# One Trainium2 core, a fused decoder layer: the load queue's order within a round is changed

## The chip, the cores and the metric

The kernel runs on one core of one Trainium2 chip. The metric is the device time of one execution in microseconds (us); of several runs the median is given. The engines are named as in the profile: PE is TensorE, DVE is VectorE, ACT is ScalarE, POOL is GpSimd, SP is SyncE, which here computes nothing and only issues DMA transfers in the order in which its program lists them ("SPq" in the rows).

## What is computed

A decoder layer of pre-norm form over 128 sequences of 64 tokens with 128 features, all in float32:

```python
x = x + self_attention(layernorm(x))        # 16 heads of 8, rotary positions, causal
x = x + cross_attention(layernorm(x), ctx)  # no softmax; followed by its own layer norm
x = x + expert_ffn(layernorm(x))            # 8 experts, each token goes to the one of largest affinity
```

`x` and `ctx` are each 128 x 64 x 128. The self-attention has a softmax. The cross-attention multiplies its unnormalised scores into the values, adds its input, and normalises. The expert layer is 128 -> 512 -> 128 with a ReLU, and its result is gated by a sigmoid.

## The kernel before

**Tiling.** The 8192 tokens are cut into 32 groups (`NG = 32`) of 256 tokens, four sequences each. For the two attentions each group passes through all engines in pieces, and the pieces are software-pipelined by hand: every engine runs a loop of rounds, and in round c it does the piece of group c, another piece of group c-1, and so on back to group c-8. A call `stage(g, k, op)` in a function `one(g)` means "in this round, do `op` for the group k behind". Each engine executes its own list strictly in order; semaphores tie the lists together. Almost every tile has two buffers, used by even and odd groups (`g.par`), so a transfer into a buffer waits until the group two before has finished with it.

After the rounds comes the expert part: 71 blocks of 128 tokens, fetched from a DRAM table sorted by expert.

**The load queue.** SP's list is the subject. In round c it issues, in the version before:

- `load_again` (L519 to L525): group c-4's x a second time, into `xr`, for the residual sum `x1_sum` (DVE, L1514). It waits for `x1_sum` of group c-6.
- `load_x` (L512 to L518): group c's x into `xin`. It waits until ACT's `norm_x` (L1046) of group c-2 has read the buffer. The first reader is DVE's `stats_x` (L1341, shown as `stat_L<-xin`) in DVE's round c.
- `by_head` (L533 to L541): four transfers that copy group c-1's rotated queries and keys `qk` into head slots `ex`. They wait for POOL's `rotated` (L1927, tile `qk`) of group c-1, which is the last piece of POOL's round c. The first reader is PE's `max_scores` (L706).
- `load_ctx` (L526 to L532): group c's context into `cin`. It waits for PE's `ctx_turned` (L782) of group c-2. The first reader is `ctx_turned` of group c.
- then, in `late_loads(c)`, whatever is due once: constants in round 0; ten transfers of biases and cross-attention weights in round 1 (L493 and L495); the mask and four constants in round 4 (L500 to L503); one transfer of 256 KB of expert weights in each of rounds 10 to 25.

**How the rounds of the engines stand.** PE's numbering is one ahead: PE's round c+1 runs beside DVE's, ACT's and POOL's round c (PE does `max_scores` of the group 4 behind, DVE reduces its result 3 behind). One such round is about 14 us long in the middle of the run.

Order on DVE in one round, as far as it matters: `weighted_turned` (L1491), `choose`, `inverse`, two maxima (L1481), small routing steps, `rotate` (L1461), `stats_x` (L1341, `xin`), `x1_sum` (L1514), `stats_x1`, `y_sum` (L1541), `partners` (L1471); then POOL's `rotated`.

Order on PE: `max_scores` (L696, L706), `ctx_turned` (L782), `x_turned` (L664), `values` (L683), ..., `queries_keys` (L673), `max_rows` (L720), `scores` (L738 to L752), `projected` (L800, what `x1_sum` waits for), `attended`, `values_keys`, `cross_output` (L877 to L884), `weighted` (L769). `cross_output` reuses a bank that `x1_sum` of the group behind it has to have read: L877 waits for it.

Two one-time places: PE's `constants()` (L654 to L656, after `queries_keys` of group 1) waits for the ten transfers of SP's round 1 and for masks that ACT makes; and at the end of DVE's round 4 `setup` reduces the mask (L1741, tile `pen`) and waits for its transfer.

Of the kernel before, what the change touches and what calls it, by code (L numbers as in the profile page):

```python
# [144 lines left out]
def decoder_kernel(nc, x, ctx, mask, wself, wcross, bcol, brow, cent, w1t, lngb, b1c, w2t, b2r,  # L145
# [17 lines left out]
    with es:  # L163
# [254 lines left out]
        def stage(g, back, op, *args):  # L418

            if g.back(back).within(NG):  # L420
                op(g.back(back), *args)

        def rounds(one, count, early=None):

            for i in range(count):
                one(Group(i))
                if early:
                    early(i)
# [50 lines left out]
        def _(sp):  # L479
# [61 lines left out]
                    sp.dma_start(ex[g.par][i:P:4, i, :, :], qk[g.par][i:P:4, :, :]).then_inc(d_by[g.par], 16)  # L541

            def one(g):
                stage(g, 4, load_again)
                stage(g, 0, load_x)
                stage(g, 1, by_head)
                stage(g, 0, load_ctx)
            rounds(one, NG + 4, early=late_loads)


# [1618 lines left out]
```

## Time and profile before

| | us |
|---|---|
| median of 3 runs | 671.95 |
| the runs | 669.51, 671.95, 680.21 |
| the profiled execution, device time | 673.08 |
| its span, first to last instruction | 670.6 |
| PE busy in it | 548.1 |

The profiled execution is 1.1 us over the median, and 2.5 us of it lie outside the span. In the profile a bracket behind a row of a timeline gives the engine's idle time just before that row and what released it. PE's rounds from 86 to 465 us are the even part of the run; 0 to 86 us is the filling of the pipeline with the one-time loads; from about 475 us on the expert blocks run.

### The profile page before, as it was taken

To read this page: it belongs to the slowest core of one execution; us is meant where nothing else is said; L and a number is where in the kernel's file an instruction comes from. 1 tells how busy PE (TensorE), PEld (TensorE's weight loads), DVE (VectorE), ACT (ScalarE), POOL (GpSimd) and SP (SyncE) were. 2 spreads that over 40 slices of the span, in tenths; PEclk is the share of its full clock that TensorE was granted. 3 is DMA by queue.
4 is the path that set the end of the run, shared out by engine and by line. 5 is a ranking of instruction groups with operands and counts; after the bars stand their busy time and mean duration, and the time that the engine had idled before them with its cause. 6 is when DMAs were issued, how large, how long until landed. Compare 5 with 4: busy or idle time off the path is not lost.

```text
span 670.6 us, 26792 instructions
## 1 busy us (share of the span) xinstructions
PE 548.1 (82%) x8783; PEld 444.6 (66%) x8783; DVE 490.5 (73%) x1701; ACT 439.2 (65%) x1496; POOL 388.6 (58%) x659
## 2 busy tenths in 40 slices
PE   2284787989998788988889888888788798899995
PEld 1163565767776566665666666666578797799895
DVE  3282698887788777788778887898647676677674
ACT  1343366666676666667567676765567787799894
POOL 1231266676776776766677777675635655555454
PEclk9998799998899998999799999999969998899998
DMA  2215211122222322222222222111211212232220
GB/s 75 75 46 84 53 43 53 59 81 72 67 73 75 108 71 65 67 77 89 90 71 66 74 71 70 51 50 60 70 27 47 56 54 58 79 87 69 60 57 16
DMA packets 61653, 43.85 MB, mean 65 GB/s; under 512 B 17216, under 2 KB 52801, under 8 KB 61520
## 3 DMA queue, kind: packets, MB, share of 16 engines
q1 hardware_dynamic: 56304, 32.84, 17.5%
q0 software_dynamic: 4320, 8.66, 3.9%
q8 instruction: 74, 1.21, 0.8%
q10 hardware_dynamic: 896, 0.66, 0.4%
q14 instruction: 59, 0.48, 0.3%
HBM read 24.46 MB, written 9.74 MB: 51 GB/s over the span
## 4 chain that ended last, share of the span: by engine, by line
PE 39%; DVE 17%; issue 14%; SPq 10%; DMA 8%; POOL 5%; ACT 3%; ACTq 2%; DVEq 2%; another core or an unknown queue 0%; POOLq 0%
DMA xin<-in_x 8%; PE side L970 7%; SPq L541 5%; PE side L955 4%; PE quad L955 4%; PE quad L738 3%; DVE mx L1481 3%; POOL qk L1927 3%; SPq L530 2%; PE quad L752 2%; PE quad L706 2%; PE side L769 2%; DVE x L1514 1%; PE quad L939 1%; PE side L800 1%
## 5 line engine op out<-in xcount | busy, mean ns | idle before, releaser
L2047 POOL DMA_INDIRECT out<-yo,rb x71 | 69.7, 981 | 76.7 <-DVE yo L1808 49.6
L1088 ACT ACTIVATE prob<-quad 128x1024 f32<-128x1024 f32 x64 | 65.6, 1026 | 65.9 <-PE quad L752 65.9
L970 PE MATMUL side<-w,hT 128*128 x568 | 79.0, 284 | 9.9 <-DVE hT L1613 7.1
L2015 POOL DMA_INDIRECT expert_rows<-pay,sli x64 | 64.3, 1004 | 34.4 <-DVE sli L1652 22.2
L970 PEld LDWEIGHTS side<-w,hT 128*128 128x128 f32 x568 | 71.4, 197 | 12.3 <-issue 12.3
L1481 DVE TENSOR_REDUCE mx<-quad 128x16 f32<-128x1024 f32 x64 | 73.9, 1195 | 4.1 <-PE quad L706 3.9
L1916 POOL TENSOR_TENSOR rs_L<-ve_L,half 128x2 f32<-128x2 f32 x32 | 22.3, 698 | 62.6 <-ACT ve_L L1148 62.6
L752 PE MATMUL quad<-shift,pick 32*128 32x128 bf16 x512 | 30.3, 221 | 30.8 <-issue 30.0
L1341 DVE BATCH_NORM_STATS2 stat_L<-xin 128x6 f32<-128x128 f32 x64 | 15.5, 284 | 51.2 <-DMA xin<-in_x 50.9
L1935 POOL TENSOR_TENSOR mt<-mx,mt 128x32 bf16<-128x32 f32 x64 | 14.8, 252 | 53.7 <-ACT mt L1081 53.7
L752 PEld LDWEIGHTS quad<-shift,pick 32*128 32x128 bf16 x512 | 15.8, 92 | 43.9 <-issue 43.6
L1603 DVE TENSOR_SCALAR xh<-rb 128x128 f32<-128x128 f32 x71 | 24.5, 346 | 26.6 <-issue 24.8
L1219 ACT COPY w1b<-w 128x512 f32 x71 | 43.6, 615 | 0.3 <-issue 0.3
L955 PE MATMUL quad<-xhT,w1b 128*128 128x128 f32 x288 | 39.8, 283 | 1.9 <-ACT xhT L1197 1.9
L955 PE MATMUL side<-xhT,w1b 128*128 128x128 f32 x280 | 38.3, 281 | 0.9 <-ACT xhT L1197 0.9
L769 PE MATMUL side<-prob,vau 128*32 128x64 f32 x2048 | 38.1, 229 | 1.1 <-ACT prob L1088 1.0
L738 PE MATMUL quad<-ex,qk 32*64 32x256 f32 x1024 | 35.9, 386 | 3.6 <-issue 2.9
L706 PE MATMUL quad<-ex,qk 32*64 32x256 f32 x1024 | 38.4, 405 | 0.0
L955 PEld LDWEIGHTS quad<-xhT,w1b 128*128 128x128 f32 x288 | 36.5, 199 | 2.1 <-ACT xhT L1197 2.0
L1197 ACT ACTIVATE xhT<-quad,gb 128x128 f32<-128x128 f32 x71 | 33.1, 466 | 7.2 <-PE quad L939 7.0
L683 PE MATMUL side<-ws,xT 128*128 128x128 f32 x128 | 21.2, 290 | 20.1 <-issue 16.0
L673 PE MATMUL side<-xT,ws 128*128 128x256 f32 x128 | 36.9, 413 | 0.6 <-ACT xT L1053 0.6
(280 smaller groups left out, 1737.6 us busy)
## 6 DMA issues: line engine op xcount, KB each, us to landing
ex<-qk SPq DMA_DIRECT2D x128, 64.0 KB
rb<-expert_rows SPq DMA_DIRECT2D x71, 68.0 KB
xin<-in_x SPq DMA_DIRECT2D x32, 128.0 KB
cin<-in_ctx SPq DMA_DIRECT2D x32, 128.0 KB
xr<-in_x SPq DMA_DIRECT2D x32, 128.0 KB
w<-in_w1t SPq DMA_DIRECT2D x8, 256.0 KB
w<-in_w2t SPq DMA_DIRECT2D x8, 256.0 KB
out<-yo,rb POOLq DMA_INDIRECT x71
```

Source lines behind the costliest of these rows:

```text
L673: last = mm(BANK["queries_keys"][:, i * TG:(i + 1) * TG], w, xT[g.par][:, :], start=True, stop=True)
L706: last = mm(quad[64 * b:64 * b + 64, r_, 256 * j:256 * j + 256], qk[g.par][strip, 0, own], ex[g.par][strip, :, 1, own], start=False, stop= ...
L738: mm(quad[64 * b:64 * b + 64, r_, 256 * j:256 * j + 256], qk[g.par][strip, 1, own], ex[g.par][strip, :, 0, own], start=j == 0, stop=False, ...
L752: last = mm(quad[:, r_, :].rearrange("p (j i q) -> p j i q", j=J, i=4)[:, :, i, :], pick[strip, i, :, :].rearrange("p b k -> p (b k)"), sh ...
L769: last = mm(to[32 * i:32 * i + 32, j, :, r_, :], vau[g.par][:, j, 4 * r_ + i, :], prob[g.par][:, r_, (4 * j + i) * SQ:(4 * j + i + 1) * SQ ...
L955: last = mm(HT[u][c // 2][:, (c % 2) * P:(c % 2 + 1) * P], w1b[u][:, c * P:(c + 1) * P], xhT[u][:, :], start=True, stop=True)
L970: last = mm(YB[u][:, 0:D], hT[u][:, c, :], w2[:, bass.ds(e, 1), c, :], start=c == 0, stop=c == FC - 1)
L1088: act(prob[g.par][:, 2 * h_:2 * h_ + 2, :], quad[:, 2 * h_:2 * h_ + 2, :], ACT.Exp).then_inc(*ac_a.done(f"e{h_}"))
L1219: cp(w1b[u][:, :], w1[:, bass.ds(e, 1), :].rearrange("p e f -> p (e f)")).then_inc(*ffn["act_w1"].done("act_w1"))
L1481: v.tensor_reduce(mx[g.par][:, 2 * h_:2 * h_ + 2, :], quad[:, 2 * h_:2 * h_ + 2, :].rearrange("p r (h k) -> p r h k", k=SQ), AX.X, ALU.max ...
L2015: v.indirect_dma_start(out=rows, out_offset=bass.IndirectOffsetOnAxis(ap=sli[g.par][:, j:j + 1], axis=0), in_=pay[g.par][:, j, :], in_offs ...
L2047: v.indirect_dma_start(out=o_rows, out_offset=bass.IndirectOffsetOnAxis(ap=number, axis=0), in_=yo[b.c % 4][:, :], in_offset=None, bounds_ ...
```

## The change

SP's list of a round is put in another order, and two pieces move to another group.

```diff
             def one(g):
+                stage(g, 0, load_x)
+                stage(g, 2, by_head)
+                stage(g, 2, load_ctx)
                 stage(g, 4, load_again)
-                stage(g, 0, load_x)
-                stage(g, 1, by_head)
-                stage(g, 0, load_ctx)
             rounds(one, NG + 4, early=late_loads)
```

In round c the queue now issues x of group c first; then the head-slot transfers and the context of group c-2 (before: c-1 and c); then the second x of group c-4; then what `late_loads(c)` has. No transfer, no wait inside a function and no other engine's list is changed.

## Rows read from the trace of the kernel before

**Rows 1.** The page: busy time, share of the span and instructions of each engine.

```profile
PE 548.1 (82%) x8783; PEld 444.6 (66%) x8783; DVE 490.5 (73%) x1701; ACT 439.2 (65%) x1496; POOL 388.6 (58%) x659
```

**Rows 2.** The page: the chain that ended last, its shares by line.

```profile
DMA xin<-in_x 8%; PE side L970 7%; SPq L541 5%; PE side L955 4%; PE quad L955 4%; PE quad L738 3%; DVE mx L1481 3%; POOL qk L1927 3%; SPq L530 2%; PE quad L752 2%; PE quad L706 2%; PE side L769 2%; DVE x L1514 1%; PE quad L939 1%; PE side L800 1%
```

**Rows 3.** Waits, 80 to 440 us: total us, times, longest.

```profile
DVE stat_L L1341 <- DMA xin<-in_x: 39.6, 20, 3.1
...
PE side L877 <- DVE x L1514: 9.9, 11, 1.3
```

**Rows 4.** Waits of the SP queue, 86 to 480 us.

```profile
SPq L130 <- POOL qk L1927: 264.1, 28, 17.3
```

**Rows 5.** Timeline of SP, start: start us, us issuing, transfer, count.

```profile
3.26 0.43 SPq L516 DMA_DIRECT2D xin<-in_x  x1
22.60 2.44 SPq L541 DMA_DIRECT2D ex<-qk  x4
...
28.60 2.90 SPq L495 DMA_DIRECT2D wop<-in_wself  x4
...
47.01 2.91 SPq L541 DMA_DIRECT2D ex<-qk  x4
...
61.56 0.47 SPq L500 DMA_DIRECT2D mk<-in_mask  x1
```

**Rows 6.** Timeline of PE, start.

```profile
32.94 0.79 PE L654 MATMUL side<-ws,bvx 128*128 128x128 f32 x2 [9.95 <-DMA wop<-in_wself]
...
34.86 2.01 PE L706 MATMUL quad<-ex,qk 32*64 32x256 f32 x32
...
71.76 1.20 PE L683 MATMUL side<-ws,xT 128*128 128x128 f32 x4 [13.15 <-issue]
```

**Rows 7.** Timeline of ACT, start: the last of the masks.

```profile
24.34 0.30 ACT L1040 CAST tri_b<-cf 128x128 bf16<-128x128 f32 x1
```

**Rows 8.** Timeline of DVE, start.

```profile
33.91 0.49 DVE L1341 BATCH_NORM_STATS2 stat_L<-xin 128x6 f32<-128x128 f32 x2 [9.22 <-DMA xin<-in_x]
...
68.18 1.22 DVE L1741 TENSOR_REDUCE pen<-mk 128x64 f32<-128x1024 int32 x1 [11.32 <-DMA mk<-in_mask]
...
70.95 0.70 DVE L1491 STREAM_TRANSPOSE ot<-side 128x512 f32<-128x512 f32 x1
```

**Rows 9.** Timeline of SP, one round of the middle.

```profile
285.08 2.38 SPq L541 DMA_DIRECT2D ex<-qk  x4
287.51 0.58 SPq L530 DMA_DIRECT2D cin<-in_ctx  x1
...
288.65 0.43 SPq L523 DMA_DIRECT2D xr<-in_x  x1
289.12 0.47 SPq L516 DMA_DIRECT2D xin<-in_x  x1
```

**Rows 10.** Timeline of DVE, the same round.

```profile
293.57 0.49 DVE L1341 BATCH_NORM_STATS2 stat_L<-xin 128x6 f32<-128x128 f32 x2 [2.38 <-DMA xin<-in_x]
...
294.27 0.42 DVE L1514 TENSOR_TENSOR x<-side,xr 128x256 f32<-128x256 f32 x1
```

**Rows 11.** Timeline of ACT, the same round: `norm_x`.

```profile
281.76 0.69 ACT L1046 ACTIVATE xn<-xin,rs_L 128x128 f32<-128x128 f32 x2
```

**Rows 12.** Timeline of PE: two starts of L769, and a `ctx_turned`.

```profile
127.99 1.10 PE L769 MATMUL side<-prob,vau 128*32 128x64 f32 x64
...
141.03 1.10 PE L769 MATMUL side<-prob,vau 128*32 128x64 f32 x64
...
298.30 0.44 PE L782 MATMUL side<-cf,cin 128*128 128x128 f32 x2
```

**Rows 13.** Rounds, cut at the first issue of L541: length, busy times, PE clock, DMA.

```profile
158.34:171.80 13.46, 12.18 (x243) 9.35 (x242) 11.53 (x41) 9.46 (x36) 9.72 (x19) 1.00 0.27 80
...
255.19:270.52 15.33, 12.59 (x215) 9.71 (x221) 10.87 (x40) 9.08 (x35) 9.77 (x19) 0.78 0.24 72
...
451.80:465.48 13.68, 11.67 (x234) 8.65 (x234) 11.42 (x40) 8.59 (x32) 9.05 (x18) 1.00 0.16 51
```

## The prediction

> **What bounds the kernel now.** I read the page first. PE is the busiest engine with 82% [rows 1], so it is the engine that a faster kernel must keep fed. But the chain that ended last [rows 2] is not PE alone: its largest single part is the load of x into `xin`, 8% of the span, and the issuing of the head-slot transfers (L541, 5%) and of the context (L530, 2%) stand in it too. A transfer in that chain means that something computes only when the transfer lands, so I turned to the waits. Between 80 and 440 us DVE waits 39.6 us for x, in 20 of about 26 rounds, and PE waits 9.9 us at L877 for DVE's residual sum [rows 3]. SP spends 264 us in 28 waits for POOL's `qk` [rows 4]: whatever stands behind that wait in SP's list cannot leave before it.
>
> One round of the middle shows the loop. POOL's `qk` ends just before 285.08; the four head-slot transfers and the context take SP until 288.1; then the weights, the second x at 288.65, and x at 289.12 [rows 9]. DVE has been idle for 2.38 us when x is there, at 293.57, and the residual sum starts at 294.27 [rows 10]. From that sum DVE goes on to `partners`, POOL to the next `qk`, SP to the next x. This loop is one round long and runs through x's latency: 293.57 - 289.12 = 4.45 us from issue to use. PE idles at L877 because the sum is late.
>
> What would the round be without it? The trace has a round in which PE meets no wait for DVE: L769 starts at 127.99 and again at 141.03 [rows 12], 13.04 us; PE's short gaps that no other engine causes are in it. The 22 rounds from 158.34 to 465.48 [rows 13] take 307.1 us, 13.96 each.
>
> The start has two more such waits. PE sits 9.95 us before `constants()` for the weights that SP issued only at 28.60, behind the head slots of group 0 issued at 22.60 [rows 5, 6]; x of group 2 comes behind them, and DVE waits 9.22 us for it [rows 8]. And DVE waits 11.32 us for the mask, issued at 61.56 behind the head slots of group 3; PE's next bank waits for DVE's L1491 behind it, and PE is idle for 13.15 us until 71.76 [rows 5, 6, 8].
>
> **The change, part by part.** Nothing is added or removed; each piece moves relative to the one wait that matters, that for `qk`.
>
> *The head slots* of group c-2 in round c are the same transfers at the same moment: before, round c-1 issued them. Their wait is the end of POOL's round c-1 in both orders. New ahead of them stands only `load_x` of group c, which waits for `norm_x` of group c-2; `qk` of group c-2 itself depends on that, so the head slots never wait longer for it. Cost 0, but for 0.47 us of issue that lies in SP's idle time [rows 4, 9].
>
> *x* now stands in front of the next wait for `qk` instead of behind the previous one. Behind the slot of 285.08 comes x of the following group, held by `norm_x`, which in this round starts at 281.76, 3.3 us before the next `qk` ends [rows 11, 9]. In the new order it would leave at 282.5 where it left at 289.12: 6.6 us earlier, against a lateness of 2.38. It is hidden, with some 4 us to spare. If that cover fell short, each us missing would be a us of the loop.
>
> *The context* left three rounds ahead of its use and now leaves one ahead: the slot at 287.51 will carry the group that PE turns at 298.30 [rows 9, 12], 10.8 us later, 9.8 in a 13 us round. x, the last of this round's burst, is in use 4.45 us after its issue. Cost 0.
>
> *The second x* leaves 0.5 us earlier than at 288.65, since the weights now come after it. It has 5.6 us until its use at 294.27 and was never waited for. With x in time the sum wants it up to about 1.6 us earlier (2.38 of the wait, less what PE's own L800 holds back), at 292.7, 4.5 us after the issue at 288.1. That is just x's latency of 4.45 with 256 KB less ahead of it, so I take 0, with bounds 0 and 0.5 us a round.
>
> *The 22 rounds.* Going from 13.96 to 13.04 saves 0.92 x 22 = 20.3 us. Bounds: at least the 9.9 us that PE loses at L877 [rows 3], at most the 20.3. The open question is the clock. In the round 255.19 to 270.52 the granted clock is 0.78 of full, and it is 15.33 us long against 13.96 [rows 13]; it stayed at the lower of the two levels, 1.2 GHz, for part of it, after PE had idled several times. The rounds with such a fall are part of the 13.96. I keep 4 us, about three such excesses of 1.4, for falls and single waits that happen anyway, and take 20.3 - 4 = 16.3 us.
> The Trainium skill, TensorE: Matmul & The Clock Gate, section "HAM oscillation — how this bites in real kernels", says that waits for DMA between bursts of matmuls make the array fall back to its slower clock. By that rule fewer waits mean fewer falls, and the 4 us would be gained as well, for a total 4 us lower; the trace agrees for the round shown, and no row shows what falls remain when x is in time.
>
> *The rounds before 158 us* are five. Their waits for x are among those of rows 3, but DVE has setup work in them, and I have no round of theirs without it to compare with. I take 0.
>
> *Weights of round 1.* SP's round 1 now holds x of group 1 and then the ten transfers; nothing waits, so they start at about 3.2 instead of 25.7, and their 6 us of issue ends near 9. `constants()` then waits for ACT's masks, done at 24.64 [rows 7], not for transfers: 8.3 us earlier than 32.94. Behind it L706 waits for the head slots of group 0, whose last issue starts at about 24.4; with 3.6 to 4.9 us to land (x's 4.45, less or more for the burst ahead) it starts at 28.0 to 29.3 instead of 34.86 [rows 5, 6]. What follows on DVE and PE moves alike: 6.8 us saved, bounds 5.5 and 8.3. x of group 2 leaves near 12.5, when `norm_x` of group 0 is done, so DVE's 9.22 us go too; they ran beside PE's wait and count once. The context of group 0 leaves at 25 instead of 1.3 and is needed after L706, at 30: 5 us, enough.
>
> *The mask* moves from behind the head slots of group 3 (58.5) to behind those of group 2 (47.01), the context and the second x: it is issued near 51.1 instead of 61.56 [rows 5]. It took 68.18 - 61.56 = 6.6 us; with one more transfer ahead I allow 7.2, so it lands at 58.3 on the old clock. DVE gets there at 68.18 - 11.32 = 56.86. The wait shrinks from 11.3 to 1.4: 9.9 us saved, bounds 8 and 11.3. PE's idle 13.15 us shrinks as much. After an idle time of this length PE's clock starts at the lower level; what one fall costs is the 1.4 us of the round 255.19 (15.33 less 13.96), and with a short idle time it is gained: 1.4, bounds 0 and 1.9.
>
> *The expert part* waits for nothing that SP's rounds decide. 0.
>
> **Sum**, against the profiled execution's 673.1: 6.8 + 9.9 + 1.4 + 16.3 = 34.4, so 638.7; its time stands 1.1 over the median of the runs shown, so I predict 638.
>
> **The rivals.** A. The start is repaired, but the middle gives back most: the second x, or the path from the maxima to L720, is the next late thing, and the round falls only to about 13.6. Then the middle gives the 22 x 0.36 = 8 us, total 26: 646. For it: the second x had only about as much slack as x was late, and L720 hangs on DVE's maxima through ACT and POOL. Against: a round of 13.04 exists, with that path in it.
> B. The start alone gains, the middle nothing, for instance because more falls of the clock eat it: 18.1 us, 654.
> C. Little changes: DMA transfers of the start are limited by their number, the early burst of ten delays ACT's constants by the 6 us it wins, and the middle behaves as in B: 10 us, 662. Rows 5 to 7 speak against it, since those constants are used only after 15 us.
> D. Slower: the context, now one round ahead, comes late and PE stops at L782 each round. It has 9.8 us; the gain of 34 is used up when it is late by 1.1 us in each of 32 rounds, so from a landing of 10.9 us on. At 12 us the time would be 672 - 34 + 70 = 708. The longest landing read in the rows is the mask's 6.6 us.
>
> **From these to numbers.** My forecast 0.50 (628 to 642), A 0.25, B 0.12, C 0.09, D 0.04. 2% of 672 is 13.4 us, about what a measurement of this kernel can tell from no change: faster means under 658.5. My forecast, A and B are faster: 0.87; C is the same, 0.10 with its edge; slower 0.03. For 8 in 10 the range takes in my forecast, A and B's upper part: 626 to 656.
>
> **What the profile after would show.** Right: no or hardly any wait of DVE on `xin`; SP's x leaving about 3 us before the head slots; L706's first use at 28 to 29; the mask's wait under 3 us; rounds of 13.0 to 13.3 us with L877 unheld and instead DVE waiting for L800. Wrong: DVE waiting for DMA `xr` at L1514 (A); PE's clock low in more rounds (B); PE or ACT waiting for `cin` (D); the first 86 us shortened by less than 15.

## The result and the profile after

| | before | after |
|---|---|---|
| median, us | 670.96 | 645.76 |
| the runs | 669.51 to 680.21 (4) | 642.80 to 648.45 (4) |
| the profiled execution | 673.08 | 645.28 |
| its span | 670.6 | 642.9 |

The ratio is 0.962, with a 95% interval of 0.956 to 0.968: the change makes the kernel 3.8% faster. The forecast was 638, in a range of 626 to 656. All ratios here go by fast executions; left out of them as slow are, on later occasions, one of the changed kernel at 1218.3 us and five of the kernel before from 677.4 to 680.5 us.

The chain that ended last is read first. It is a line of the page, with shares of the span:

```profile
PE side L970 7%; PE quad L738 5%; PE quad L706 4%; PE side L769 4%; PE quad L752 4%; PE side L673 4%; PE side L955 3%; PE quad L955 3%; PE side L830 3%; PE side L866 3%; DVE mx L1481 3%; PE side L884 2%; PE side L800 2%; DVE hT L1613 2%; PE side L683 2%
```

x, SP's L541 and the context, in front in [rows 2], are gone. Of the 15 parts shown, 13 are PE's: the kernel has become bound by its busiest engine. The waits of 80 to 430 us say the same (total us, times, longest):

```profile
DVE x L1514 <- PE side L800: 41.6, 25, 2.2
...
PE side L720 <- POOL mt L1935: 1.1, 6, 0.3
```

No wait for a transfer is among them. DVE's 39.6 us for x and PE's 9.9 us at L877 [rows 3] have vanished, and DVE now waits for PE in 25 rounds. It is the sign that the prediction named for a round set by PE.

SP and DVE in one of the even rounds (timeline):

```profile
258.52 2.38 SPq L541 DMA_DIRECT2D ex<-qk  x4
260.94 0.58 SPq L530 DMA_DIRECT2D cin<-in_ctx  x1
261.57 0.47 SPq L523 DMA_DIRECT2D xr<-in_x  x1
262.08 0.47 SPq L509 DMA_DIRECT2D w<-in_w1t  x1
262.60 0.44 SPq L516 DMA_DIRECT2D xin<-in_x  x1
```
```profile
263.69 0.48 DVE L1341 BATCH_NORM_STATS2 stat_L<-xin 128x6 f32<-128x128 f32 x2
...
265.95 0.42 DVE L1514 TENSOR_TENSOR x<-side,xr 128x256 f32<-128x256 f32 x1 [1.57 <-PE side L800]
...
276.37 0.47 DVE L1341 BATCH_NORM_STATS2 stat_L<-xin 128x6 f32<-128x128 f32 x2
```

The list looks like that of [rows 9], but the x at 262.60 belongs to the group of the next round. `stat_L` at 263.69 reads the x that left a round before and has no bracket: it did not wait. The x of 262.60 is read at 276.37, 13.8 us after its issue. The sum at 265.95 waited for PE's L800, not for `xr` issued at 261.57.

The start, SP, then PE, then DVE:

```profile
3.25 0.47 SPq L493 DMA_DIRECT2D br<-in_brow  x1
...
12.40 0.39 SPq L516 DMA_DIRECT2D xin<-in_x  x1
22.82 2.46 SPq L541 DMA_DIRECT2D ex<-qk  x4
...
42.31 0.47 SPq L500 DMA_DIRECT2D mk<-in_mask  x1
```
```profile
24.99 0.77 PE L654 MATMUL side<-ws,bvx 128*128 128x128 f32 x2 [1.79 <-ACT tri_b L1040]
26.89 1.92 PE L706 MATMUL quad<-ex,qk 32*64 32x256 f32 x32
...
52.85 1.19 PE L683 MATMUL side<-ws,xT 128*128 128x128 f32 x4 [2.96 <-issue]
```
```profile
49.26 1.22 DVE L1741 TENSOR_REDUCE pen<-mk 128x64 f32<-128x1024 int32 x1 [1.12 <-DMA mk<-in_mask]
```

The weights are there before ACT's masks, PE goes on at 26.89 instead of 34.86 [rows 6], the mask's wait is 1.12 us instead of 11.32 [rows 8], and PE idles 2.96 us instead of 13.15.

Rounds, cut at the first issue of L541 as in [rows 13]:

```profile
258.52:271.19 12.67, 11.33 (x238) 8.78 (x237) 10.66 (x40) 9.30 (x36) 9.71 (x19) 1.00 0.28 86
...
298.44:312.63 14.19, 12.94 (x221) 10.28 (x226) 9.90 (x39) 8.84 (x34) 9.75 (x19) 0.76 0.25 79
312.63:326.78 14.15, 12.79 (x268) 9.82 (x250) 11.60 (x41) 9.77 (x37) 9.72 (x19) 1.00 0.25 76
```

An undisturbed round is now 12.67 us. But where the clock falls (0.76 of full in the second row), that round and the next take 14.19 and 14.15, 3.0 us more for the two. Not every long round is the clock's: the one from 394 to 409 us takes 14.71 at full clock, and the same round takes 14.6 to 14.7 us in the kernel before and in every profile below but the three with the scatters moved.

Where the 27.7 us of the span came from: the head slots of group 9 leave at 158.34 before and 139.98 after, so the start gave 18.4 us. From there to the head slots of group 31 pass 307.1 us before (to 465.48) and 297.7 after (437.69 - 139.98): the 22 rounds gave 9.4. The rest takes 205.1 and 205.2 us.

### The profile page after: what moved, and what is told of

Read it like the earlier page. It is cut to its first block, busy times and chain, and to the rows that moved or that the text cites. A ratio compares the mean times of both kernels' runs of the same rounds, so it can differ in the third digit from the quotient of the medians.

```text
span 642.9 us, 26792 instructions
## 1 busy us (share of the span) xinstructions
PE 548.1 (85%) x8783; PEld 444.9 (69%) x8783; DVE 481.6 (75%) x1701; ACT 438.5 (68%) x1496; POOL 388.5 (60%) x659
## 3 DMA queue, kind: packets, MB, share of 16 engines
q1 hardware_dynamic: 56304, 32.84, 18.1%
## 4 chain that ended last, share of the span: by engine, by line
PE 64%; issue 14%; DVE 13%; ACT 3%; ACTq 2%; DVEq 2%; POOL 1%; another core or an unknown queue 1%; POOLq 0%
PE side L970 7%; PE quad L738 5%; PE quad L706 4%; PE side L769 4%; PE quad L752 4%; PE side L673 4%; PE side L955 3%; PE quad L955 3%; PE side L830 3%; PE side L866 3%; DVE mx L1481 3%; PE side L884 2%; PE side L800 2%; DVE hT L1613 2%; PE side L683 2%
## 5 line engine op out<-in xcount | busy, mean ns | idle before, releaser
L752 PE MATMUL quad<-shift,pick 32*128 32x128 bf16 x512 | 30.7, 221 | 32.9 <-issue 32.0
L1514 DVE TENSOR_TENSOR x<-side,xr 128x256 f32<-128x256 f32 x31 | 13.2, 425 | 54.2 <-PE side L800 54.2
L752 PEld LDWEIGHTS quad<-shift,pick 32*128 32x128 bf16 x512 | 15.9, 92 | 45.9 <-issue 45.6
L1955 POOL TENSOR_TENSOR rs_T<-ve_T,half 128x2 f32<-128x2 f32 x32 | 22.3, 698 | 29.1 <-ACT ng L1155 27.4
L955 PE MATMUL quad<-xhT,w1b 128*128 128x128 f32 x288 | 38.3, 276 | 1.4 <-issue 1.4
L769 PE MATMUL side<-prob,vau 128*32 128x64 f32 x2048 | 38.1, 229 | 1.1 <-ACT prob L1088 1.0
L738 PE MATMUL quad<-ex,qk 32*64 32x256 f32 x1024 | 36.0, 386 | 3.5 <-issue 2.5
L706 PE MATMUL quad<-ex,qk 32*64 32x256 f32 x1024 | 38.2, 403 | 0.6 <-issue 0.6
L673 PE MATMUL side<-xT,ws 128*128 128x256 f32 x128 | 37.6, 419 | 0.6 <-ACT xT L1053 0.6
L769 PEld LDWEIGHTS side<-prob,vau 128*32 128x32 f32 x2048 | 32.4, 116 | 5.9 <-ACT prob L1088 1.5
```

Of the source, the lines that this page charges most:

```text
L673: last = mm(BANK["queries_keys"][:, i * TG:(i + 1) * TG], w, xT[g.par][:, :], start=True, stop=True)
L706: last = mm(quad[64 * b:64 * b + 64, r_, 256 * j:256 * j + 256], qk[g.par][strip, 0, own], ex[g.par][strip, :, 1, own], start=False, stop= ...
L738: mm(quad[64 * b:64 * b + 64, r_, 256 * j:256 * j + 256], qk[g.par][strip, 1, own], ex[g.par][strip, :, 0, own], start=j == 0, stop=False, ...
L752: last = mm(quad[:, r_, :].rearrange("p (j i q) -> p j i q", j=J, i=4)[:, :, i, :], pick[strip, i, :, :].rearrange("p b k -> p (b k)"), sh ...
L769: last = mm(to[32 * i:32 * i + 32, j, :, r_, :], vau[g.par][:, j, 4 * r_ + i, :], prob[g.par][:, r_, (4 * j + i) * SQ:(4 * j + i + 1) * SQ ...
L955: last = mm(HT[u][c // 2][:, (c % 2) * P:(c % 2 + 1) * P], w1b[u][:, c * P:(c + 1) * P], xhT[u][:, :], start=True, stop=True)
```

## The experiments

One measure is used through all of them. In each profile I take the length of the 22 rounds from group 9 to group 31, and how long PE's granted clock stood at its lower level in them, added up over windows of 1 us. The window in which the stretch ends is counted whole, which makes the sum up to 0.9 us too long (most in the third profile of the changed kernel).

**x alone.** The kernel before, with only x moved a round ahead:

```diff
             def one(g):
+                if g.n == 0:
+                    load_x(g)
                 stage(g, 4, load_again)
-                stage(g, 0, load_x)
+                stage(g, -1, load_x)
                 stage(g, 1, by_head)
                 stage(g, 0, load_ctx)
```

> x of the next group one round earlier, every other piece of the queue where it was before (one-time loads too). My account of the result: the start keeps both stalls (the weights' 9.95 us of PE, the mask's 11.3 us of DVE), the 22 even rounds behave as after the change, about 13.5 us each with no wait for x. 671 less about 10 us: 661 (657 to 664). If the gain of the middle came from the head slots or the context instead of x, the time stays at 671.

Measured: 664.5 us against 669.8 of the kernel before on that chip, 0.989 (0.982 to 0.996): a gain, but a small one. The waits, of PE and DVE from 0 to 80 us and of DVE from 150 to 430 us (lines lie 2 lower here):

```profile
PE side L656 <- DMA wop<-in_wself: 10.1, 1, 10.1
...
DVE pen L1743 <- DMA mk<-in_mask: 11.3, 1, 11.3
...
DVE x L1516 <- PE side L802: 23.0, 15, 2.1
DVE x L1516 <- DMA xr<-in_x: 10.2, 6, 2.1
```

The start keeps both stalls, as expected (group 9 leaves at 157.1), and the wait for x is gone in the middle. The head slots and the context need not move for that. The 22 rounds took 302.8 us with 44.2 us of low clock. The time is at the edge of what was expected, 0.5 us over it: more falls than I knew of. The last line is new: here the second x does come late, 10.2 us in six rounds. In this order it stands behind the weights; in the changed kernel it stands ahead of them and is never waited for.

**One-time loads late.** The changed kernel, with what rounds 1 and 4 issue once put behind the next head slots:

```diff
-            rounds(one, NG + 4, early=late_loads)
+            def one_time(i):
+                if i not in (1, 4):
+                    late_loads(i)
+                if i in (2, 5):
+                    late_loads(i - 1)
+            rounds(one, NG + 4, early=one_time)
```

> The changed kernel, but the one-time transfers of rounds 1 and 4 (weights; mask and constants) are issued one head-slot wait later, where the kernel before had them. My account: the start loses 17 to 18 us again, the middle keeps its gain: 646 + 18 = 664 (660 to 667), with waits of about 8 us at L654 for wop and about 11 us at L1741 for the mask. If x alone repaired the start, it stays below 650.

Measured: 661.4 us, 0.985 (0.979 to 0.991) of the kernel before. The time is within what was expected. PE waits 10.1 us for `wop` and DVE 11.9 us for the mask again. Group 9 leaves at 158.65, where three profiles of the changed kernel have 137.4 to 140.2: 18.5 to 21.2 us, the whole gain of the start. x of group 2 was early here and repaired none of it.

**The mask alone late.** The same edit for round 4 only.

> The changed kernel, but the mask and the four constants of round 4 are issued behind the head slots of group 3 again; the weights of round 1 keep their early place. My sum priced the mask at 9.9 us (11.3 with the clock after the idle time) and the weights at 6.8. Expected about 11 us over the changed kernel: 654 (651 to 658), with the weights' wait at L654 under 2 us and the mask's wait at L1741 near 11 us. If the mask's wait hides beside something else in the new order, it costs under 5 us.

Measured: 657.8 us (656.9 to 665.2), 0.986 (0.977 to 0.995) of the kernel before, in the expected range. Waits of DVE, then of PE, 0 to 80 us (lines lie 6 lower here):

```profile
DVE pen L1747 <- DMA mk<-in_mask: 12.0, 1, 12.0
...
PE side L660 <- ACT tri_b L1046: 1.9, 1, 1.9
```

`wop` no longer holds PE; the wait at the place of L654 is ACT's 1.9 us. Group 9 leaves at 149.15: the mask costs 9.0 to 11.7 us, and the weights of round 1 the other 9.5.

**The numbers alone.** The kernel before, order kept, with `by_head` and `load_ctx` moved to the group 2 behind:

```diff
-                stage(g, 1, by_head)
-                stage(g, 0, load_ctx)
+                stage(g, 2, by_head)
+                stage(g, 2, load_ctx)
```

> The kernel before with only the two numbers changed: head slots and context of group c-2, the order in the list left as it was (second x, x, head slots, context, one-time transfers). My account: what counts is that x stands ahead of a qk wait that comes a round later; where the second x stands is immaterial, so 646 (640 to 650), with x never waited for. If the place of the second x matters (here it goes behind the 256 KB of weights), DVE waits for xr at L1514 and the time is over 652.

Measured: 643.3 us, 0.963 (0.957 to 0.968): the changed kernel's time. So the gain comes from the two numbers; that the list is also reordered adds nothing that these runs show. My wording of this test had a slip: with this order the second x is issued behind the weights of one round, but also a whole round earlier than in the changed kernel, so it is early, and the run does not test a late second x. That DVE waits for L800 33.8 us in 21 rounds, and never for `xr`, fits.

**The changed kernel again, and again.** Two more profiles, on two other occasions.

> The changed kernel again, for a second profile on this chip. If the falls of PE's clock in the rounds (30.6 us at the lower level in the first profile, 17.0 before the change) depend on chance, their places differ between the two profiles; if they belong to the program, they are the same to a round. Time 643 to 649 either way.

> The changed kernel once more, beside scatter_over on one chip, and a third profile. By the rule found, the 22 even rounds less half of the low clock in them take 282.3 us (280.5 to 283.5), whatever the falls are; time 640 to 647.

Measured: 641.5 and 650.1 us; the two profiled executions have 635.2 and 645.5. Both medians lie outside what was expected (643 to 649, and 640 to 647), by 1.5 and 3.1 us. Most of the falls lie elsewhere each time: from 140 us on they begin near 199, 277, 305, 346, 373 and 431 us in the first profile, 169, 210 and 251 in the second, 172, 227, 254, 333, 374 and 432 in the third.

**The kernel before again.**

> The kernel before, for a second profile. In the profiles read so far the 22 even rounds, less half of the time that PE's clock stood at its lower level in them, take 298.6 us before the change (307.1 less 17.0 / 2) and 280.7 to 282.4 in the four kernels or profiles where x leaves a round earlier. If that rule holds, this profile gives 298 to 299 again, whatever its falls are. If the 298.6 was one profile's chance, it misses by over 3 us.

Measured: one execution, 675.4 us. The 22 rounds took 309.1 us with 30.6 us of low clock, which gives 293.8, not 298 to 299. Together:

| profile | 22 rounds, us | at the lower clock, us | rounds less half of it |
|---|---|---|---|
| before | 307.1 | 17.0 | 298.6 |
| before, again | 309.1 | 30.6 | 293.8 |
| after | 297.7 | 30.6 | 282.4 |
| after, again | 292.5 | 20.4 | 282.3 |
| after, third | 297.9 | 34.0 | 280.9 |
| x alone | 302.8 | 44.2 | 280.7 |
| one-time loads late | 298.4 | 34.0 | 281.4 |
| mask late | 301.8 | 37.4 | 283.1 |
| numbers alone | 296.6 | 27.2 | 283.0 |

With x in time the last column stays within 280.7 to 283.1 while the low clock varies from 20.4 to 44.2 us. So in these kernels the difference from profile to profile is the clock, each low microsecond costing half a microsecond, as it must where PE sets the pace: 1.2 GHz is half of 2.4. For the kernel before the rule does not hold: its two profiles differ by 4.8 us. PE waits for DVE there, so part of a slow stretch may cost nothing, and taking off half of it would take off too much; two profiles do not show it. My expectation for this run failed by that.

**The scatters moved, first try.** The falls of the clock in these 22 rounds of the changed kernel's first profile all begin at L752 or within 2 us behind it, where PE stops two or three times for 0.3 to 0.5 us without any engine as releaser. The kernel before has these stops too. PE and, beside it, POOL:

```profile
250.69 0.21 PE L752 MATMUL quad<-shift,pick 32*128 32x128 bf16 x1 [0.34 <-issue]
251.41 0.27 PE L752 MATMUL quad<-shift,pick 32*128 32x128 bf16 x4 [0.51 <-issue]
252.13 0.33 PE L752 MATMUL quad<-shift,pick 32*128 32x128 bf16 x8 [0.46 <-issue]
```
```profile
249.34 1.06 POOL L2015 DMA_INDIRECT expert_rows<-pay,sli  x1 [0.86 <-DVE sli L1652]
250.71 0.96 POOL L2015 DMA_INDIRECT expert_rows<-pay,sli  x1 [0.30 <-issue]
```

POOL issues its two scatters at that time. The edit puts them at the end of POOL's round:

```diff
                 stage(g, 3, max_low)
-                stage(g, 7, scatter_rows, 0)
-                stage(g, 7, scatter_rows, 1)
                 stage(g, 5, offset_x1)
...
                 stage(g, 1, rotated)
+                stage(g, 7, scatter_rows, 0)
+                stage(g, 7, scatter_rows, 1)
```

> The changed kernel with POOL's two scatters of a round issued after rotated instead of in the middle. In the even rounds PE has three gaps of about 0.5 us at L752 (1.3 us a round), right while POOL issues the two scatters, and every fall of the clock begins there. Theory 1: the scatters cause the gaps. Then the gaps leave L752 and appear about 6 us later in the round (L769 to L706 or L673), of the same size, and falls begin elsewhere. Theory 2: the gaps belong to L752's matmuls. Then they stay. Time within 8 us of 646 under both, lower if the gaps shrink.

Measured: 678.1 us, 1.013 (1.007 to 1.019) of the kernel before. The time is over 20 us outside what was expected (within 8 us of 646). L752 in one row, and waits of DVE and of PE, 150 to 440 us:

```profile
266.61 0.39 PE L752 MATMUL quad<-shift,pick 32*128 32x128 bf16 x16
```
```profile
DVE pay L1553 <- DMA expert_rows<-pay,sli: 39.5, 19, 2.9
```
```profile
PE side L720 <- DVE cnt L1631: 32.4, 12, 3.0
```

Its sixteen matmuls run in 0.39 us without a gap, where they needed over 2 us. (They take 0.39 us in the changed kernel as well as long as no scatter has been issued, at 44.44 for instance.) They belong to the scatters then, not to L752. They did not reappear in the place where the scatters now run, beside PE's large matmuls from L683 to L673, which I had expected. The time got worse because DVE now waits for the scatters, and PE for DVE. The clock was not helped: it was low for 58.1 us of these 22 rounds.

**Second try.** One scatter after `rotated`, one after the next round's `divide`; `x2_sum`, `stats_x2`, `var_x2` and `std_x2` later in their rounds.

> The changed kernel with POOL's two scatters moved to where PE runs its large matmuls (one after rotated, the other after the next round's divide), and the sum that waits for them (L1553), its statistics and ACT's variance moved behind rotate, so that nothing waits for the scatters. The first try of this kind (after rotated alone) took the gaps at L752 away but made DVE wait 39.5 us for the scatters. If the gaps of 1.3 us a round are caused by the scatters and worth their size, even rounds fall from 12.7 to 11.5 to 12.2 us and the time to 615 to 635. If DVE or ACT takes over as the bound, rounds stay near 12.7 or above and the time is 640 or more.

Measured: 642.2 us, 0.960 (0.956 to 0.965); rounds of about 13.4 us, no gaps within L752. PE's waits, 150 to 430 us, ACT's in the same stretch, and PE at the start of one fall of the clock:

```profile
PE side L720 <- issue: 18.7, 19, 1.3
PE quad L752 <- ACT shift L1071: 15.1, 21, 1.0
```
```profile
ACT y L1172 <- POOL sc L1975: 54.1, 21, 3.1
```
```profile
264.32 0.28 PE L720 MATMUL side<-ident_b,mt 128*128 128x64 bf16 x4 [1.33 <-issue]
...
266.80 0.61 PE L752 MATMUL quad<-shift,pick 32*128 32x128 bf16 x16 [0.80 <-ACT shift L1071]
```

The second branch of the expectation: PE waits at L752 for ACT, which waits for the variances' root (L1975) that I had moved back on POOL. At L720 the profile names no releaser, but POOL's `mt` ends at 264.22, 0.1 us before it. DVE also waits 11.0 us for the scatters. And although the gaps are gone, the clock still falls: six times in the 22 rounds, 20.5 us in all, each time within 0.4 us of the start of L752 (here at 266.7). The rounds less half of that are 286.6 us, so this kernel's rounds are held by more than PE.

**Third try.** Both scatters after `rotated`, and:

```diff
-                stage(g, 6, scaled_scores)
-                stage(g, 6, token_ids)
                 stage(g, 5, cross_queries)
                 stage(g, 3, max_by_head)
-                stage(g, 6, var_x2)
                 stage(g, 3, cross_keys_values)
                 stage(g, 3, exp, 0)
+                stage(g, 6, scaled_scores)
+                stage(g, 6, token_ids)
+                stage(g, 6, var_x2)
...
-                stage(g, 6, x2_sum)
...
                 stage(g, 7, slots)
+                stage(g, 1, rotate)
                 stage(g, 4, turned_back)
+                stage(g, 6, x2_sum)
                 stage(g, 6, stats_x2)
-                stage(g, 1, rotate)
-                stage(g, 6, affinities)
                 stage(g, 0, stats_x)
                 stage(g, 4, x1_sum)
                 stage(g, 4, stats_x1)
+                stage(g, 6, affinities)
...
-                stage(g, 6, std_y)
-                stage(g, 4, divide)
                 stage(g, 3, max_low)
+                stage(g, 4, divide)
+                stage(g, 6, std_y)
```

The three parts are ACT's, DVE's and POOL's list.

> The changed kernel with both scatters after rotated, as in the first try, and the work around them reordered: POOL does max_low before divide and the variances' root; DVE does rotate ahead of turned_back and of the sum that waits for the scatters; ACT does the scaled scores after the first exponential. In the try before this one the gaps at L752 were gone, but PE waited 0.8 us a round there for ACT and 0.6 us at L720 for POOL, in rounds of 13.4 us. If those two waits were what held the round, it falls to 11.6 to 12.2 us and the time to 615 to 630; if it stays at 13 or more, DVE, ACT and POOL together bound it and the gaps at L752 cost nothing that a better order could win.

Measured: 624.0 us (620.3 to 628.3), 0.926 (0.917 to 0.934) of the kernel before, and 4.0% under the changed kernel, which had 650.1 on the same chip. The time is within the 615 to 630 expected. It is the fastest version. The stretch of its even rounds, and what PE waits for in it:

```profile
150.00:418.00 268.00, 232.13 (x4954) 181.27 (x4939) 248.34 (x831) 195.60 (x733) 203.20 (x378) 1.00 0.26 78
```
```profile
PE side L877 <- DVE x L1514: 17.9, 20, 1.3
PE side L720 <- POOL mt L1935: 8.1, 10, 0.9
```

PEclk stands at 1.00 over those 268 us: the clock never falls in them. The rounds take 12.2 to 13.1 us, though (two at the end 14.1 and 13.3), not the 11.6 to 12.2 hoped for: DVE is busy 248 of 268 us and has become the bound, and PE waits for it at L877 again. The 22 rounds take 280.6 us. The changed kernel's 281 to 283 with the clock's part taken off is the same: the gaps were traded for waits for DVE. What was won is the clock's part, in the one profile of this kernel: the rounds are 17.3 us shorter than the 297.9 of the third profile of the changed kernel, and its profiled execution is 17.2 us faster (628.3 against 645.5).

## Why the prediction was right, and where it was off

**The mechanism** was right in its main parts. x behind a `qk` wait set the round; a round ahead it is hidden. It is hidden with more to spare than forecast: the prediction let x be held by the `norm_x` that starts at 281.76 and leave about 3 us before the head slots, 6.6 us earlier than before. But `load_x` of group c waits for `norm_x` of group c-2, and the one for that x starts a round earlier, at 266.45. So x leaves right behind the burst before: at 262.60, 8.6 us before the head slots of 271.19. The slip cost nothing. The context and the head slots cost nothing: no profile of a kernel with the change has a wait for `cin` (rival D), and for `xr` only x alone has one that counts, 10.2 us, besides 0.3 us once in the third try (rival A). ACT's masks were not delayed by the early weights: L654 starts at 24.99 (rival C).

**The start** was forecast at 18.1 us and gave 18.4 in the profile shown. Its terms: the weights at 6.8, measured 8.0 at L706; the head slots of group 0 were in use at 26.89, 1.6 us after the last of their four issues ended at 25.28, about 2.2 us after it began, not the 3.6 to 4.9 us I had carried over from x at the end of a larger burst. The mask's wait fell by 10.2 us where 9.9 was forecast. The 1.4 us for the clock was not earned; it came out as a loss of 1.1. The low clock behind the wait shrank from 13.7 us to 6.8, but before it had stood mostly in PE's idle time, where it cost nothing. The same work, from L683 to the start of L738, took 6.18 us before (71.76 to 77.94) and takes 7.31 now (52.85 to 60.16). That 18.1 and 18.4 agree so well is in part luck: the 1.2 us by which the weights gave more, and smaller gains beside them, made up for it.

**The middle** is the term that was mis-sized: 16.3 forecast, 9.4 measured in this profile (14.6 in the second one, 9.2 in the third). The step that failed is the 4 us kept for the falls of the clock. Half of the 30.6 us at the lower clock is 15.3 us, 11 more than was kept. The rounds with that taken off are 282.4 us where 22 x 13.04 = 286.9 was forecast, so 4.5 us of it came back: an undisturbed round was 12.67. By the last column of the table the gain at full clock is 11 to 18 us, which holds the forecast; the column is rough for the kernel before. But the falls did not shrink with the waits: 20.4 to 34.0 us of low clock in three profiles of the changed kernel against 17.0 and 30.6 before. And once PE sets the pace, each low microsecond costs its full half. That is rival B's mechanism, at some 7 us of its 16, beside my own. Rival A's numbers, rounds of 13.6 us and 646 in all, are the ones measured (297.7 / 22 = 13.5, and 645.8), but by luck: neither the second x nor L720 (1.1 us of waits) is what its rounds were lengthened by. The measured time lies in the range because the range took in A's, not in the 628 to 642 of my own forecast.

The rule of the Trainium skill that I had set beside it, that waits for DMA between bursts of matmuls make the clock fall (TensorE: Matmul & The Clock Gate, "HAM oscillation — how this bites in real kernels"), is not met in the direction that I drew from it. DVE's 39.6 us of waits for x went, and PE's 9.9 us for DVE with them, and the low clock did not become less. Nor does the round shown in [rows 13] bear it out: its clock falls near 263.7, behind the gaps at L752 (260.8 to 262.3), before PE's wait for DVE at L877 has begun.

The gaps at L752 are not the whole of it either. In the third try, without them, there was no fall from 140 to 420 us, though PE waited 18 us at L877 in single waits of up to 1.3 us. But the second try has no gaps within L752, and there the clock fell six times; the first has none and was low for 58.1 us, with waits of PE of up to 3 us. What makes the clock fall stays open, and so does why it did not fall in the third try, and at which rounds the falls come.

## What to carry to other kernels

In a hand-ordered load queue, ask of each transfer which wait it stands behind, not only how far ahead it is asked for. A load whose own condition is met early must stand in front of a wait that is met at the end of every round, and one-time loads too; here two numbers in the list gave 3.7%.

When a wait is removed and the busiest engine becomes the bound, what that engine had hidden counts in full: its clock, and gaps for which the profile names no engine. Take two or three profiles before a few microseconds between two orders are explained.

## What the runs showed of the hardware

Two indirect scatters issued by POOL slow PE's issue of many small matmuls: sixteen matmuls at L752 take over 2 us beside them and 0.39 us otherwise, in the even rounds, 1.1 to 1.3 us a round. The same scatters beside PE's large matmuls (L683 to L673) left no gap. Three other placements of the scatters agree on this. Through what they act was not tried.
